# A conditioned residual on one core: the weight table stored by channel, and one loop of four batches per engine with two loads in flight

## The reference

```python
# x: (64, 128, 2048) float32, condition: (64,) int in 0..15, weights: (16, 128, 128) float32
W = weights[condition]                          # (64, 128, 128), one matrix per batch
out = x + jnp.einsum('bct,bcd->bdt', x, W)
```

## Time and profile before

| | us |
|---|---|
| median of 3 runs | 325.06 (324.98 to 325.37) |
| the profiled execution, its time | 324.97 |
| its span, first to last instruction | 323.2 |

### The profile page before, as it was taken

The page is one execution under the profiler, slowest core; times in us unless marked ns, Lnnn a source line. Parts: engine busy times, 40 slices in busy tenths (PEclk is TensorE's granted clock), DMA queues, the critical chain, the costliest instruction groups (busy, mean ns, idle before and its releaser), DMA issues.

```text
span 323.2 us, 2326 instructions
## 1 busy us (share of the span) xinstructions
PE 240.3 (74%) x512; PEld 101.3 (31%) x512; DVE 146.6 (45%) x64; ACT 0.2 (0%) x1; POOL 19.0 (6%) x69
## 2 busy tenths in 40 slices
PE   0029999999999986867996869866688786878000
PEld 0014444444444432322342323322233332333000
DVE  0003766766757752555173552543545254553200
ACT  0000000000000000000000000000000000000000
POOL 0011100101001000000010000000000000000000
PEclk9999999999999998999597997999899798899755
DMA  7999999999999999999999999999999999999996
GB/s 279 382 414 422 422 425 429 428 424 430 426 428 430 425 431 426 427 431 426 429 428 427 430 425 428 430 425 430 428 427 430 426 429 428 426 430 426 429 430 284
DMA packets 17940, 135.30 MB, mean 419 GB/s; under 512 B 1042, under 2 KB 1042, under 8 KB 1554
## 3 DMA queue, kind: packets, MB, share of 16 engines
q10 hardware_dynamic: 9234, 68.16, 49.9%
q1 hardware_dynamic: 8704, 67.11, 49.7%
HBM read 68.16 MB, written 67.11 MB: 419 GB/s over the span
## 4 chain that ended last, share of the span: by engine, by line
DMA 69%; PE 20%; DVE 2%; issue 1%; ACTq 0%; POOLq 0%; DVEq 0%; ACT 0%; SPq 0%; POOL 0%
DMA out<-x_ring 59%; PE product L114 20%; DMA weight_table<-weights 6%; DMA x_ring<-x 5%; DVE x_ring L138 2%; POOLq L90 0%; ACTq L147 0%; ACTq L145 0%; DVEq L138 0%; ACT weight_table L149 0%; ACTq L144 0%; SPq L72 0%; POOLq L92 0%; SPq L84 0%; POOLq L97 0%
## 5 line engine op out<-in xcount | busy, mean ns | idle before, releaser
L114 PE MATMUL product<-x_ring,chosen_weights 128*128 (+1 forms) x512 | 240.3, 629 | 58.6 <-POOL chosen_weights L92 23.2
L138 DVE TENSOR_TENSOR x_ring<-product,x_ring 128x2048 f32 x64 | 146.6, 2291 | 154.7 <-PE product L114 154.7
L114 PEld LDWEIGHTS product<-x_ring,chosen_weights 128*128 128x128 f32 x512 | 101.3, 201 | 196.7 <-issue 196.7
L92 POOL COPY chosen_weights<-weight_table 128x128 f32 x64 | 18.8, 293 | 243.1 <-issue 125.2
L149 ACT MOVE_SHAPE weight_table<-weights x1 | 0.2, 160 | 1.4 <-PEq L166 1.4
L166 POOL MEMSET const-float32-0.0<- 128x1 f32 x1 | 0.1, 98 | 0.1
L166 POOL MEMSET const-bfloat16-1.0<- 128x1 bf16 x1 | 0.1, 101 | 0.0
L166 POOL MEMSET const-uint8-127<- 128x1 uint8 x1 | 0.1, 101 | 0.0
L166 POOL MEMSET const-float32-1.0<- 128x1 f32 x1 | 0.1, 98 | 0.0
L166 POOL BASE_LOAD x1 | 0.0, 17 | 0.2 <-issue 0.2
## 6 DMA issues: line engine op xcount, KB each, us to landing
x_ring<-x SPq DMA_DIRECT2D x32, 2048.0 KB, 16.3
out<-x_ring ACTq DMA_DIRECT2D x32, 2048.0 KB, 38.6
condition_row<-condition ACTq DMA_DIRECT2D x1, 0.2 KB
weight_table<-weights ACTq DMA_DIRECT2D x1, 0.5 KB, 18.8
```

The source lines that it names most:

```text
L92: pool.tensor_copy(chosen_weights[b][:, :], weight_table[:, bass.ds(state * features, features)]).then_inc(weights_chosen, 1)
L114: last = pe.matmul(product[:, b % psum_slots, m * BANK_COLUMNS:(m + 1) * BANK_COLUMNS], chosen_weights[b][:, :], x_ring[:, bass.ds(ring_co ...
L138: dve.tensor_tensor(tile, product[:, b % psum_slots, :], tile, AluOpType.add).then_inc(sum_done, 1)
```

## The change

The host lays the table out by channel, then state, then feature, so that a partition's part is one row of 8 KB, and the load of the table is a plain copy of 128 rows. ACT issues it ahead of the conditions.

Every engine has one loop over 16 turns of four batches (two groups), without a first turn written out. The waits that would have nothing to wait for in the first turns are met by increments that the engines make at their start: SP raises `x_loaded` by 16 and `room_free` by 16 x 4, POOL raises `weights_free` by 4, DVE raises `psum_free` by 2. The ring still holds 8 groups, now as four turns of two.

Two loads may be in flight instead of four, and two stores instead of four: a load waits for the load two groups before it, a store for the store two groups before it. There are four `chosen_weights` buffers instead of eight, and POOL is told by VectorE (`weights_free`, raised when VectorE has seen the product done) when one is free.

```diff
-BATCHES = 2
-STEPS = 4
-RING_TURNS = 2
+GROUP = 2
+IN_FLIGHT = 2
+RING_TURNS = 4
...
         @block.sync
         def _(sp):
-            for u in range(STEPS):
-                load(0, u)
-
-            with sp.Fori(1, RING_TURNS) as turn:
-                for u in range(STEPS):
-                    sp.wait_ge(x_loaded[u], 16 * turn)
-                    load(turn, u)
-            with sp.Fori(RING_TURNS, turns) as turn:
-                for u in range(STEPS):
-                    sp.wait_ge(x_loaded[u], 16 * turn)
-                    sp.wait_ge(out_stored[u], 16 * (turn - RING_TURNS + 1))
-                    load(turn, u)
+            for g in range(IN_FLIGHT):
+                sp.sem_inc(x_loaded[g], 16)
+                sp.sem_inc(room_free[g], 16 * RING_TURNS)
+            with sp.Fori(0, turns) as turn:
+                for g in range(IN_FLIGHT):
+                    sp.wait_ge(x_loaded[g], 16 * (turn + 1))
+                    sp.wait_ge(room_free[g], 16 * (turn + 1))
+                    sp.dma_start(ring_group(turn, g), dram_group(x, turn, g)
+                                 ).then_inc(x_loaded[g], 16)
...
         @block.gpsimd
             pool.wait_ge(condition_loaded, 16)
             pool.wait_ge(table_loaded, 16)
+            pool.sem_inc(weights_free, per_turn)
+            with pool.Fori(0, turns) as turn:
+                for b in range(per_turn):
+                    pool.wait_ge(weights_free, turn * per_turn + b + 1)
...
         @block.tensor
+            with pe.Fori(0, turns) as turn:
+                for b in range(per_turn):
+                    g, within = divmod(b, GROUP)
+                    if within == 0:
+                        pe.wait_ge(x_loaded[g], 16 * (turn + 2))
+                    pe.wait_ge(weights_chosen, turn * per_turn + b + 1)
+                    pe.wait_ge(psum_free, turn * per_turn + b + 1)
...
         @block.vector
+            dve.sem_inc(psum_free, psum_slots)
...
+                    dve.wait_ge(product_done, turn * per_turn + b + 1)
+                    dve.sem_inc(weights_free, 1)
                     dve.tensor_tensor(tile, product[:, b % psum_slots, :], tile,
-                                      AluOpType.add).then_inc(sum_done, 1)
+                                      AluOpType.add).then_inc(psum_free, 1)
...
         @block.scalar
-            act.dma_start(weight_table[:, :].rearrange("c (s d) -> c s d", s=states),
-                          weights.rearrange("s c d -> c s d")).then_inc(table_loaded, 16)
+            act.dma_start(weight_table[:, :], weights.rearrange("c s d -> c (s d)")
+                          ).then_inc(table_loaded, 16)
             act.dma_start(condition_row[0:1, :], condition.rearrange("(o b) -> o b", o=1)
                           ).then_inc(condition_loaded, 16)
...
+            with act.Fori(0, turns) as turn:
+                for g in range(IN_FLIGHT):
+                    act.wait_ge(room_free[g], 16 * (turn + RING_TURNS))
+                    act.wait_ge(psum_free, turn * per_turn + (g + 1) * GROUP + psum_slots)
+                    act.dma_start(dram_group(out, turn, g), ring_group(turn, g)
+                                  ).then_inc(room_free[g], 16)
+            for g in range(IN_FLIGHT):
+                act.wait_ge(room_free[g], 16 * (turns + RING_TURNS))
...
-        "weights": np.ascontiguousarray(L0_cond_weights),
+        "weights": np.ascontiguousarray(np.asarray(L0_cond_weights).transpose(1, 0, 2)),
```

More of the change, by code:

```diff
@@ L26, in conditioned_residual @@
     batches, channels, time = x.shape
-    states, _, features = weights.shape
-    turns = batches // (STEPS * BATCHES)
-    group = BATCHES * time
+    _, states, features = weights.shape
     matmuls = time // BANK_COLUMNS
     psum_slots = PSUM_BANKS // matmuls
+    per_turn = IN_FLIGHT * GROUP
+    turns = batches // per_turn
+    group_columns = GROUP * time
     with ExitStack() as ctx:
@@ L38, in sem @@
             return ctx.enter_context(nc.semaphore(name))
-        x_ring = sbuf("x_ring", [channels, RING_TURNS * STEPS * group])
+        x_ring = sbuf("x_ring", [channels, RING_TURNS * IN_FLIGHT * group_columns])
         weight_table = sbuf("weight_table", [channels, states * features])
-        chosen_weights = [sbuf(f"chosen_weights{b}", [channels, features]) for b in range(STEPS * BATCHES)]
+        chosen_weights = [sbuf(f"chosen_weights{b}", [channels, features]) for b in range(per_turn)]
         condition_row = sbuf("condition_row", [1, batches], condition.dtype)
@@ L70, in _ @@
         def _(sp):
-            def load(turn, u):
-                sp.dma_start(ring_group(turn, u), batches_of(x, turn, u)).then_inc(x_loaded[u], 16)
-            for u in range(STEPS):
-                load(0, u)
-            with sp.Fori(1, RING_TURNS) as turn:
-                for u in range(STEPS):
-                    sp.wait_ge(x_loaded[u], 16 * turn)
-                    load(turn, u)
-            with sp.Fori(RING_TURNS, turns) as turn:
-                for u in range(STEPS):
-                    sp.wait_ge(x_loaded[u], 16 * turn)
-                    sp.wait_ge(out_stored[u], 16 * (turn - RING_TURNS + 1))
-                    load(turn, u)
+            for g in range(IN_FLIGHT):
+                sp.sem_inc(x_loaded[g], 16)
+                sp.sem_inc(room_free[g], 16 * RING_TURNS)
@@ L96, in _ @@
             pool.wait_ge(condition_loaded, 16)
             pool.wait_ge(table_loaded, 16)
[L98 to L104, removed]
+            pool.sem_inc(weights_free, per_turn)
+            with pool.Fori(0, turns) as turn:
+                for b in range(per_turn):
+                    pool.wait_ge(weights_free, turn * per_turn + b + 1)
+                    state = pool.value_load(condition_row[0:1, bass.ds(turn * per_turn + b, 1)],
+                                            min_val=0, max_val=states - 1)
+                    pool.tensor_copy(chosen_weights[b][:, :],
+                                     weight_table[:, bass.ds(state * features, features)]
+                                     ).then_inc(weights_chosen, 1)
@@ L106, in _ @@
         @block.tensor
         def _(pe):
[L108 to L128, removed]
+            with pe.Fori(0, turns) as turn:
[5 more added lines that the diff above has]
+                    pe.wait_ge(psum_free, turn * per_turn + b + 1)
+                    for m in range(matmuls):
+                        last = pe.matmul(
+                            product[:, b % psum_slots, m * BANK_COLUMNS:(m + 1) * BANK_COLUMNS],
+                            chosen_weights[b][:, :],
+                            x_ring[:, bass.ds(ring_column(turn, g) + within * time + m * BANK_COLUMNS,
+                                              BANK_COLUMNS)],
+                            start=True, stop=True)
+                    last.then_inc(product_done, 1)
@@ L130, in _ @@
         @block.vector
         def _(dve):
+            dve.sem_inc(psum_free, psum_slots)
             with dve.Fori(0, turns) as turn:
[L133 to L137, removed]
+                for b in range(per_turn):
+                    g, within = divmod(b, GROUP)
+                    tile = x_ring[:, bass.ds(ring_column(turn, g) + within * time, time)]
+                    dve.wait_ge(product_done, turn * per_turn + b + 1)
+                    dve.sem_inc(weights_free, 1)
@@ L138, in _ @@
                     dve.tensor_tensor(tile, product[:, b % psum_slots, :], tile,
-                                      AluOpType.add).then_inc(sum_done, 1)
+                                      AluOpType.add).then_inc(psum_free, 1)
         @block.scalar
         def _(act):
-            def store(turn, u):
-                act.wait_ge(sum_done, turn * (STEPS * BATCHES) + (u + 1) * BATCHES)
-                act.dma_start(batches_of(out, turn, u), ring_group(turn, u)).then_inc(out_stored[u], 16)
+            act.dma_start(weight_table[:, :], weights.rearrange("c s d -> c (s d)")
+                          ).then_inc(table_loaded, 16)
@@ L157, in _ @@
-            for u in range(STEPS):
-                act.wait_ge(out_stored[u], 16 * turns)
+            with act.Fori(0, turns) as turn:
[6 more added lines that the diff above has]
+                act.wait_ge(room_free[g], 16 * (turns + RING_TURNS))
```

21 lines of the change are left out of this document (11 added, 10 removed).

## The result

| | us |
|---|---|
| median, the changed kernel (16 runs) | 324.58 (323.69 to 324.94) |
| median, the kernel before, run beside it (16 runs) | 325.56 (324.76 to 326.18) |
| ratio | 0.9965, 95% interval 0.9954 to 0.9976 |
| profiled execution after: its time, its span | 324.94, 323.2 |

The change makes the kernel 0.35% faster, 0.8 to 1.5 us of 325.56. The forecast was 1.3 us off an execution of 324.97. But the two profiled executions have the same span, 323.2 us: this one is the slowest of its kernel's 16, and the one before (324.97) lies with the fastest of its own. That makes them a good pair to read, since what was gained in one stretch must have been lost in another.

The account below looks back on a forecast made before the run. The kernel was taken as bound by moving 135.30 MB at 428 GB/s, 316.1 of 323.2 us. Terms of 1.0 + 0.2 + 0 + 0 + 0, with 0.1 for smaller items, saved 1.3: 323.7 us, range 322.7 to 325.1.

Parts of the forecast that it names:

- rival A: Table load: two queues reading at once, not the table's rows, give 392 GB/s; 324.4 to 325.1, say 324.8; chance 0.18.
- Rival D: End: load queue waits less, DMA engines end closer together; up to 1 us more saved, 322.5; chance 0.05.
- Term 1: Table load beside x: 8 KB rows restore the rate from 392 GB/s; 1.0 us saved, lower bound 0.
- Term 2: Head: table issued first, two queues feed the ramp from the start; 0.2 us saved, bounds 0 and 0.9.
- Terms 3 and 4: Arithmetic starting 11 us sooner, and two transfers in flight instead of four: each worth 0.
- Term 5: Tail: the last group's product and sum stay covered by remaining stores, with 3 to 5 us to spare; worth 0.
- rivals B and C: Two transfers in flight run dry, 331.7 or 326.1, chance 0.07; the last group's sums come uncovered, 328.1, chance 0.05.

Follow-up runs that it names:

- e1: The kernel before with only the table laid out by channel in 8 KB rows, still issued after the conditions: 324.44 us, ratio 0.9965.
- e2: The changed kernel with the table by state again, in 512 B pieces, still issued first: 325.77 us, ratio 1.0006 to the kernel before.
- e9: The changed kernel with the table in 2 KB pieces, four states side by side per channel: 324.80 us, ratio 0.9974 to the kernel before.
- e8: The changed kernel without the programs of POOL, PE and DVE; loads, table and stores stay: 322.53 us, ratio 0.9904 to the kernel before.
- e14: The changed kernel with 24 more semaphore increments on DVE behind each sum, 1536 in all: 326.89 us, ratio 1.0047 to the kernel before.
- e6: The changed kernel with the last group stored as two transfers of one batch each, over 128 partitions: 323.69 us, ratio 0.9945 to the kernel before.
- e3: The changed kernel with four loads and four stores in flight, turns of eight batches: 324.35 us, ratio 0.9972 to the kernel before.
- e5: The changed kernel with its last batch stored in two transfers, 120 partitions and 8: 325.06 us, ratio 0.9983 to the kernel before.
- e4: The kernel before with two loads and two stores in flight and four buffers of chosen weights: 325.58 us, ratio 1.0006.

## Why the prediction was right, point by point

- **Bound and sum.** Right: the transfer at 428 GB/s bounds both kernels; the forecast of 1.3 us saved lies in the measured 0.8 to 1.5. Between medians it is 0.98. The range of 322.7 to 325.1 was wide enough to hold rival A's time too; what tells the forecast from A is e1 and e2, not the total. The 323.7 was set against an execution of 324.97; the 16 runs beside the changed kernel have their median at 325.56, so 0.6 of the 0.9 us between 323.7 and 324.58 is the start and not the change. (Rival D's sum comes to 322.7, not 322.5.)
- **Term 1**, 1.0 us: measured 1.0 in the stretch (392 to 425 GB/s over 13 us) and 1.1 by e1. Its reason, the size of the pieces in memory, is shown by e1, e2 and e9; the prediction named the 2 KB packets as well, and e9 shows that these are not it.
- **Term 2**, 0.2 us: the ramp's shortfall fell by 0.26 with the whole change. But e1, with the old order of issues, has 343 GB/s there and 0.2 of it, so that it came mostly with the table's rows too. SP's first load went out at 1.56, 0.76 us later than before and inside the bounds, with the start unmoved.
- **Terms 3 and 4**, 0: PE started at 11.04 (forecast 10.9). The 0.8 us from last byte to semaphore was read too long: the last store landed at 322.7, 0.4 us after the last byte at 322.3. Nothing hung on it. The load queue waits for loads alone, 252.9 us in 30 waits; loads land 19.5 us after issue, and from 34 us to the last stores nothing ran dry.
```profile
SPq L70 <- DMA x_ring<-x: 252.9, 30, 9.2
```
- **Term 5**, 0: right in its outcome, and close in its times. Here is the changed kernel's first store, its landing, and the last group's product and sum:
```profile
11.04 21.32 PE L97 MATMUL product<-x_ring,chosen_weights 128*128 x42 [11.04 <-DMA x_ring<-x]
...
23.99 7.22 ACTq L127 DMA_DIRECT2D out<-x_ring  x2
...
DMA to landing us min/median/max: 14.4/14.4/14.4
...
301.22 7.13 PE L97 MATMUL product<-x_ring,chosen_weights 128*128 x16 [2.68 <-DVE x_ring L114]
...
308.60 2.29 DVE L114 TENSOR_TENSOR x_ring<-product,x_ring 128x2048 f32 x1 [1.14 <-PE product L97]
```
 The first store went out at 23.99 (forecast 23.2) and took 14.4 us again, as in the earlier trace rows. The last load was issued at 281.3 and landed 19.6 us later, at 300.9, 22 us before the end (forecast 20). The last sum ended at 310.89, 10.0 us after it, and the last store was issued at 313.2, once an older one had landed, 2.3 us after the sum. So the cover was there, and rivals B and C did not come in this kernel. The sum left out a loss at the first store, 0.3 us between 19 and 34 us, which the last section comes back to.
- **What was off: the last 1.9 us, priced as fixed.** The prediction read the stretch at 85 GB/s as some DMA engines still at work and left it in both sums; only rival D spoke of it, and in the wrong direction. In this pair of executions it grew by 1.1 us and took the whole gain; over all runs the gain stands. That the total came out right although this term moves by a microsecond from one execution to the next is in part luck: it happens to move about as much in both kernels, whose runs spread over 1.4 and 1.3 us. e8 to e14 show that it grows with the number of instructions. The new loops record 2639 instead of 2326; at 1.25 ns that would be 0.4 us, less than the 1.1 us between e6 and the changed kernel at the same number, and e3 and e1 (2532 and 2325, 324.35 and 324.44) don't show it.

## What to carry to other kernels

Where the DMA engines are full from end to end, look for the stretches below the full rate and price them, not the engines' work: here a layout on the host that turns 512 B pieces into 2 KB or more was worth about 1 us, and the rewritten loops, the earlier start by 11 us and half the transfers in flight nothing that could be told. Read the last microseconds by themselves: a rate of a sixteenth of the full one is a single DMA engine left over. Here it grew with the number of instructions, even of those in an engine's idle time, and once it was nearly 4 us behind, two stores in flight were too few to hide it (e14). And take two profiled executions as two samples: their spans were equal here while the medians were 1 us apart.

## What the runs showed of the hardware that was not expected

One of the sixteen DMA engines falls behind the others, and further the more instructions were recorded: at the last landings it comes behind the fifteenth by nothing that shows with 426 and 587, by 0.5 us with 956, 1.3 with 1738, 0.8 and 1.4 with 2326 and 2325, 1.2 to 2.8 with 2480 to 2640, and in e14, with 4175, by 4.1 at 310 us. That is 0.4 to 1.3 ns for each instruction more than e8's. The spread at nearly the same number is more than a microsecond, and what makes it is open. PE alone, POOL alone and e14 each add instructions of another kind. No row names the traffic. Reads of instructions would fit, and so would the writing of the profiler's own records; every timed run here lists a span and a clock, so none without recording exists to tell them apart. Which of the sixteen it is stays open too (e5).

One sort of traffic can be seen, though it is not what grows. The kernel before and e1, with their written-out first turns, each have one packet of kind "instruction" of 16 KB in a DMA queue, at 65.7 and 55.8 us, some 0.95 us long. At the next landing the last engine's distance from the fifteenth has gone from 0.2 to 0.8 us, and from under 0.1 to 1.3. The changed kernel has no such packet. At its end the kernel before shows two late engines, 1.0 and 1.8 us behind the eighth, where the changed kernel has one, 3.0 behind.

Joining a busy queue costs time: in the kernel before the first store's first packet starts 3.7 us after issue, in the changed one 3.5, with 14.4 us to landing in both. That is 2.7 more than the even share of the rate and the fixed 1.9 make.

And the first store brings a dip in the rate, some 3 us after its issue, in every run in which it goes out by 24.1 us. In the changed kernel that is 279 GB/s for one microsecond. It needs no compute engine; e8, whose first store goes out at 10.75 us, has the deepest:
```profile
10.00:13.00 3.00, 0.00 (x0) 1.00 1.00 410
13.00:16.00 3.00, 0.00 (x0) 1.00 1.00 303
16.00:19.00 3.00, 0.00 (x0) 1.00 1.03 434
```
That is 0.9 us lost, against 0.3 in the changed kernel. In these microseconds the packets of the loads are slower, in e8 up to 798 ns each where 309 is the rule, and no packet of the store has started yet (the first does so 4.6 us after issue). The kernel before, e4 and e2, whose first stores go out at 34.1, 33.4 and 27.2 us, have no dip. So an earlier start of the stores was not free here. Its cause was not tested.
